# Flags of the unused slots read in a nest: GpSimd's additions of expert results in a two-layer graph and mixture-of-experts kernel

## The reference

```python
xn = _layernorm(x)
x = x + L0_gnn(xn, src, dst, ...) + L0_mix(xn)
x = x + L0_ffn(_layernorm(x))        # 8 experts, each row goes to the best 2
xn = _layernorm(x)
x = x + L1_gnn(xn, edges, edge_weight, ...) + L1_mix(xn)
x = x + L1_ffn(_layernorm(x))        # 1 shared expert for all rows, and 8 of which each row takes 2
```

## Time and profile before

| | us |
|---|---|
| median of 3 runs | 2321.13 (2317.22 to 2322.07) |
| the profiled execution, its own time | 2329.73 |
| its span, first to last instruction | 2328.1 |
| TensorE busy | 2124.0 (91%) |
| VectorE busy | 1713.4 (74%) |
| ScalarE busy | 1231.5 (53%) |
| GpSimd busy | 397.7 (17%) |
| mean granted clock of TensorE | 0.958 of full speed |

### The profile page before, as it was taken

One profiled execution on the slowest core, in us unless ns is written; L12 is line 12 of the kernel. 1 busy time (PEld: TensorE's weight loads), 2 busy tenths in 40 slices (PEclk: granted clock), 3 DMA queues, 4 the chain that ended last, 5 costly groups with the idle time before them and its releaser, 6 DMA issues. The chain is left out here.

```text
span 2328.1 us, 47346 instructions
## 1 busy us (share of the span) xinstructions
PE 2124.0 (91%) x18181; PEld 1978.3 (85%) x18181; DVE 1713.4 (74%) x3516; ACT 1231.5 (53%) x2864; POOL 397.7 (17%) x327
## 2 busy tenths in 40 slices
PE   4768999999868999995999999999998999999996
PEld 2458999999758999994778899989987999999996
DVE  5689778778388888885666566556656887888885
ACT  4376555555425766674541444444435225766674
POOL 4000000000024444443000000000000032444444
PEclk9888999999978999997898999999999999999998
DMA  4143333333444877787100666456642015877786
GB/s 133 60 122 87 87 107 95 87 100 102 145 141 153 229 234 232 222 226 194 29 1 24 187 189 188 129 166 188 188 127 96 24 58 164 233 233 227 224 225 167
DMA packets 236910, 338.91 MB, mean 146 GB/s; under 512 B 29305, under 2 KB 198342, under 8 KB 236550
## 3 DMA queue, kind: packets, MB, share of 16 engines
q1 hardware_dynamic: 208800, 296.14, 40.6%
q0 software_dynamic: 24432, 35.68, 8.6%
q10 hardware_dynamic: 3446, 3.97, 0.5%
HBM read 258.83 MB, written 76.90 MB: 144 GB/s over the span
## 5 line engine op out<-in xcount | busy, mean ns | idle before, releaser
L2306 PE MATMUL bank<-WB_r,XN_r 128*128 128x448 f32 x1400 | 399.7, 367 | 3.7 <-DVE WB_r L2265 3.7
L2265 DVE TENSOR_TENSOR WB_r<-WB,WB_r 128x448 fp32r<-128x448 f32 x350 | 214.0, 624 | 166.2 <-ACT WB_r L2258 166.1
L2258 ACT CAST WB_r<-WB 128x448 fp32r<-128x448 f32 x350 | 197.7, 568 | 222.2 <-PE bank L2306 217.7
L2306 PEld LDWEIGHTS bank<-WB_r,XN_r 128*128 128x128 f32 x1400 | 263.2, 188 | 26.8 <-DVE wb__r L2231 4.4
L1860 PE MATMUL bank<-SC_r,WB_r 128*128 128x256 f32 (+1 forms) x2064 | 254.8, 283 | 12.1 <-issue 9.3
L1860 PEld LDWEIGHTS bank<-SC_r,WB_r 128*128 128x128 f32 x2064 | 248.5, 191 | 16.6 <-issue 16.6
L1044 ACT CAST WB_r<-bank 128x200 fp32r<-128x200 f32 x391 | 137.8, 352 | 196.4 <-PE bank L1028 194.4
L1875 PE MATMUL bank<-R_r,H_r 128*128 128x256 f32 x1752 | 214.0, 280 | 4.6 <-DVE R_r L1771 4.6
L1875 PEld LDWEIGHTS bank<-R_r,H_r 128*128 128x128 f32 x1752 | 207.8, 188 | 4.9 <-issue 4.9
L1724 ACT ACTIVATE wb_<-bank,WB 128x256 f32<-128x256 f32 (+1 forms) x344 | 133.3, 476 | 97.3 <-issue 63.4
L1860 PE MATMUL bank<-SC_r,XN_r 128*128 128x256 f32 x1392 | 169.6, 280 | 4.2 <-issue 3.3
(11 more groups left out here) (436 smaller groups left out, 5305.4 us busy)
## 6 DMA issues: line engine op xcount, KB each, us to landing
WB<-adjw SPq DMA_DIRECT2D x350, 224.0 KB, 2.8
WB<-in_f_pack SPq DMA_DIRECT2D x127, 512.0 KB
WB<-in_f_pack SPq DMA_DIRECT2D x62, 640.0 KB
adjw<-X SPq DMA_DIRECT2D x24, 1600.0 KB, 7.6
WB<-in_f_pack SPq DMA_DIRECT2D x65, 516.0 KB
xd<-XN SPq DMA_DIRECT2D x15, 640.0 KB, 5.5
y<-X SPq DMA_DIRECT2D x10, 640.0 KB, 3.3
X<-y SPq DMA_DIRECT2D x6, 640.0 KB, 6.4
```

The lines of the kernel that those rows point to most:

```text
L2258: e.copy(split_w(m)[0], RAW[m % PR]).then_inc(S("whigh"), 1)
L2265: e.tensor_tensor(al, RAW[m % PR], ah.bitcast(F32), ALU.subtract).then_inc(S("wlow"), 1)
L2306: mm_ = e.matmul(conv_bank(k, band, c)[:, 0:PW], x[st][:, o], y, start=(st == 0 and i == 0), stop=(st == T - 1 and i == 2))
```

## The change

On GpSimd the late slots (25 and up) become a recursive nest of conditionals. In the branch for "used", the slot's two additions are issued, and then, inside that branch, the gather and the flag of the next slot follow, without waiting for the landing and without the write into `mark`. The landing of a late slot is now read from the transfers' own semaphore (`late0`, `late1`, 32 for each slot) by whoever needs it: the next addition, and VectorE before it reuses a buffer. In the branch for "unused", GpSimd waits for all late additions of the layer, counts up a new semaphore `landed` once, and issues the gathers that are left; flags of later slots aren't read. SyncE waits for `landed` at the two places above. The tile `mark` and the semaphore `added` are gone. Nothing of the other engines' handling of the slots changes.

```diff
-        late = (NSLOT - SURE) * L + max(n - SURE, 0)
-        if late:
-            e.wait_ge(S("added"), late)
-
-    def add_pool(e, L, i):
+        if n > SURE:
+            e.wait_ge(S(f"late{L}"), 32 * (n - SURE))
+
+    def wait_all_added(e, L):
+        e.wait_ge(S("add"), 32 * SURE * (L + 1))
+        e.wait_ge(S("landed"), L + 1)
+
+    def add_pool(e, L, i, sem):
         s = L * NSLOT + i
-
-        def rows_of_slot(sem):
-            wait_added(e, L, i)
-            for q in range(2):
-                e.wait_ge(S("obs"), 2 * s + q + 1)
-                e.indirect_dma_start((Y, out)[L], ..., yob[s % 2][:, q, :], None, compute_op=ALU.add).then_inc(S(sem), 16)
-
-        def run():
-            rows_of_slot(f"late{L}")
-            e.wait_ge(S(f"late{L}"), 32 * (i - SURE + 1))
-            e.memset(mark[:, :], 0.0).then_inc(S("added"), 1)
-
-        if i < SURE:
-            rows_of_slot("add")
-        else:
-            if_used(e, L, i, run, lambda: owed(e, "added", (NSLOT - SURE) * L + i - SURE, 1))
+        wait_added(e, L, i)
+        for q in range(2):
+            e.wait_ge(S("obs"), 2 * s + q + 1)
+            e.indirect_dma_start((Y, out)[L], ..., yob[s % 2][:, q, :], None, compute_op=ALU.add).then_inc(S(sem), 16)
+
+    def landed_pool(e, L, n):
+        if n > SURE:
+            e.wait_ge(S(f"late{L}"), 32 * (n - SURE))
+        e.sem_inc(S("landed"), 1)
+
+    def late_pool(e, L, i):
+        if i == NSLOT:
+            landed_pool(e, L, i)
+            return
+        if i + 4 < NSLOT:
+            gather_pool(e, L, i + 4)
+        e.wait_ge(S("used"), 2 * L + 2)
+        o = L * NSLOT + i
+        with e.If(e.value_load(filled[0:1, o:o + 1], min_val=0, max_val=1)):
+            add_pool(e, L, i, f"late{L}")
+            late_pool(e, L, i + 1)
+        with e.Else():
+            landed_pool(e, L, i)
+            for j in range(i + 5, NSLOT):
+                gather_pool(e, L, j)
 
     def slots_pool(e, L, stored):
         gather_pool(e, L, 1)
-        for i in range(NSLOT):
-            if i + 2 < NSLOT:
-                gather_pool(e, L, i + 2)
+        for i in range(SURE + 2):
+            gather_pool(e, L, i + 2)
             if i == 2:
                 stored()
             if i >= 2:
-                add_pool(e, L, i - 2)
-        add_pool(e, L, NSLOT - 2)
-        add_pool(e, L, NSLOT - 1)
+                add_pool(e, L, i - 2, "add")
+        late_pool(e, L, SURE)

     def fetch_sp(e):
-        wait_added(e, 0, NSLOT)
+        wait_all_added(e, 0)
...
         wait_out(e)
-        wait_added(e, 1, NSLOT)
+        wait_all_added(e, 1)
```

More of the change, by code:

```diff
@@ L141, in program @@
     filled = sb("filled", [1, 2 * NSLOT], I32)
-    mark = sb("mark", [1, 1])
     slot_i = sb("slot_i", [128, 2 * NSLOT], I32)
@@ L1940, in wait_added @@
             e.wait_ge(S("add"), 32 * sure)
-        late = (NSLOT - SURE) * L + max(n - SURE, 0)
-        if late:
-            e.wait_ge(S("added"), late)
-    def add_pool(e, L, i):
-        s = L * NSLOT + i
-        def rows_of_slot(sem):
-            wait_added(e, L, i)
-            for q in range(2):
-                e.wait_ge(S("obs"), 2 * s + q + 1)
-                e.indirect_dma_start((Y, out)[L], bass.IndirectOffsetOnAxis(ap=slot_i[:, 2 * i + q:2 * i + q + 1], axis=0),
-                                     yob[s % 2][:, q, :], None, compute_op=ALU.add).then_inc(S(sem), 16)
-        def run():
-            rows_of_slot(f"late{L}")
-            e.wait_ge(S(f"late{L}"), 32 * (i - SURE + 1))
-            e.memset(mark[:, :], 0.0).then_inc(S("added"), 1)
-        if i < SURE:
-            rows_of_slot("add")
-        else:
-            if_used(e, L, i, run, lambda: owed(e, "added", (NSLOT - SURE) * L + i - SURE, 1))
+        if n > SURE:
+            e.wait_ge(S(f"late{L}"), 32 * (n - SURE))
@@ new lines, in wait_all_added @@
+    def wait_all_added(e, L):
+        e.wait_ge(S("add"), 32 * SURE * (L + 1))
+        e.wait_ge(S("landed"), L + 1)
+    def add_pool(e, L, i, sem):
+        s = L * NSLOT + i
+        wait_added(e, L, i)
+        for q in range(2):
+            e.wait_ge(S("obs"), 2 * s + q + 1)
+            e.indirect_dma_start((Y, out)[L], bass.IndirectOffsetOnAxis(ap=slot_i[:, 2 * i + q:2 * i + q + 1], axis=0),
+                                 yob[s % 2][:, q, :], None, compute_op=ALU.add).then_inc(S(sem), 16)
```

## The result

| | before | after |
|---|---|---|
| median of 8 runs, us | 2319.78 (2317.22 to 2322.07) | 2312.78 (2307.2 to 2315.99) |
| ratio, with its 95% interval | | 0.9972 (0.9963 to 0.9981) |
| span of the profiled execution, us | 2328.1 | 2310.0 |
| mean granted clock | 0.958 | 0.961 |

A forecast was written before the change was run, and what follows sets the result against it. TensorE, busy 91% of the span, was taken as the bound, so GpSimd edits count only in two tails: 3.45 us in layer 0 plus 1.55 in layer 1, 5.0 off 2321.13, gives 2316.1 us, range 2311.5 to 2321.0.

The forecast's parts named there:

- Where the time is: GpSimd's late slots: marks delayed only two additions, the last of each layer, so the change acts on two tails.
- Part 1: Late slots before the last one: landing wait, mark and flag leave GpSimd's path, gathers go out sooner; gain 0.
- Part 2: Last addition of each layer: mark, flag and branch leave between landing and issue; 1.0 us in layer 0, 0.75 in layer 1.
- Part 3: End of layer 0: mark and skipped slots' flags leave between last landing and SyncE's fetch; 2.45 us won, bounds 1.6 to 2.65.
- Part 4: End of layer 1, landing to drain: 1.8 us shrinks to about 1.0 with five exit jumps; 0.8 won, bounds 0 to 1.7.
- a stall at the jumps: Layer 1's five exit jumps on GpSimd at 2.23 us each add 10.3 us: 5.3 lost, 2326.4 us; chance 0.10.
- The drain: End of layer 1: drain of 2.61 us may run from the last transfer on, hiding the gain there; 2316.9 us; chance 0.12.
- The clock's rise: Behind layer 0: rise to full clock stays put, half of 3.45 us is lost; 3.3 won, 2317.8 us; chance 0.15.
- more is won: Jumps without cost (0.8 us more) or an earlier clock rise (up to 1.7): about 6.6 won, 2314.5 us; chance 0.08.

The follow-up runs named there:

- land_first: Changed kernel, but in a used slot GpSimd waits for its additions' landing before the next gather and flag; ratio 0.9983 to the kernel before.
- exits: Changed kernel plus a count of a semaphore nobody reads at the end of each used branch; ratio 0.9981 to the kernel before.
- again: The changed kernel once more, no edit; ratio 0.9972 to the kernel before.
- flags_read: Changed kernel, but flags the nest doesn't read are loaded for nothing between last landing and count of landed; ratio 0.9982 to the kernel before.
- out_first: Changed kernel, but from slot 25 VectorE and ScalarE give slot i-1's output before splitting slot i+2's first weights; ratio 0.9956 to the kernel before.
- lean: Changed kernel with outputs ahead of the next weights' splits and no weight transfers for unused slots; 2305.66 us, ratio 0.9939 to the kernel before.
- l0_only: The nest in layer 0 alone, layer 1 keeping flags in a row, mark and landing wait; ratio 0.9977 to the kernel before.
- no_load: Changed kernel, but SyncE loads weights only if their slot's flag is 1, else counts up their semaphores; ratio 0.9964 to the kernel before.

## Why the prediction was right, and by how much it missed

- *Where the time is*: right. Only two additions and two ends were waiting for marks and flags, and only the two tails changed; between late slots the pace is as it was (12.12 us from 1053.36 to 1065.48).
- *Part 1, the gathers that move cost and give nothing*: not contradicted. Layer 0's landing was 0.86 us shorter in the pair of profiles, but the nine profiles that were sorted by the gather overlap, and the instruction packet sorts them better.
- *Part 2, issue behind the landing*: 1.0 + 0.75 forecast, 1.15 + 0.86 measured. My 0.82 for a wait and the transfer's start was 0.1 too long. The flag did go under the transfer, and `land_first` shows the price when it doesn't.
- *Part 3, end of layer 0*: 2.45 forecast, 2.56 measured (2.69 to 0.13).
- *Part 4, end of layer 1*: 0.8 forecast, 1.56 measured (1.83 to 0.27). This is the term that was mis-sized. It charged five jumps, one for each conditional, and there was one. `exits` shows that the price of a jump was nearly right (0.15 us for 0.17) and their number wrong.
- The stable terms sum to 6.1 us in place of 5.0. The rest up to 6.9 in the profiles is the shorter landing of layer 0, less 0.1 of slightly longer ones. The interval of the ratio reaches from 4.4 to 8.6 us, so 6.1 and 7.0 can't be told apart by it, nor 5.0. The landings' part isn't shown to belong to the change, and that the profiles' 6.9 comes so near to 7.0 is luck: with the landings of `again`, the tails won 4.53 and 3.35 us, 7.9 in all.
- The time was forecast as 2316.1 and is 2312.78. Of the 3.3 us between them 1.4 are the kernel before, whose median went from 2321.13 in three runs to 2319.78 in eight. The gain of 7.0 is above the 6.6 that the range was built for; the scatter allowed on both sides holds it.
- *The rivals*: a stall at the jumps didn't come; GpSimd's branches took 34 to 53 ns in the nest, and its 2 jumps out took 38. The rule of the Trainium skill (Runtime: NRT & Kernel Launch, Instruction fetch mechanics), that a taken branch to a page outside the two-page window waits for a fetch of that page, isn't contradicted by that: no branch of the nest showed a wait, and no run here shows whether one left the window. TensorE's 2227 ns look like such a fetch: in each of the twelve profiles exactly one branch takes over 1 us (1.2 to 2.8), it is TensorE's at the end of layer 0's slots, and a 16 KB packet of the queue `instruction` begins within 1.2 us of it. That the one waits for the other wasn't tried. The drain took 2607 ns whether it started 1.83 or 0.27 us behind the last landing, so it moves with its start. The clock's rise moved along with the work, and 2 us further; "more is won" by the clock, up to 1 us of it, isn't excluded.

## What to carry to other kernels

Where a tail waits for a landing, what the issuing engine does between landing and next issue is paid in full: here 0.9 to 1.2 us for a jump and a flag, and 0.8 for each unused slot that is asked. Read flags while a transfer is on its way, and ask no more once one says "unused". And look at what transfers for work that will not take place do in a tail: in the one profile in which they were issued beside the last but one addition, it took 7.8 us to land. Compare the parts of a tail from one event to the next, not spans: two profiles of one kernel differed by 1 us in a landing and by 2.5 us in the stretch between.

## What the runs showed of the hardware

- A chain of conditionals that all end at one point was left by one jump of 38 ns; with one instruction between the ends each exit took 0.23 us, 0.15 of it the jump (exits).
- GpSimd's drain at the end took 2607 ns in eleven of the twelve profiles and 2686 in one (flags_read, where it also began 0.4 us behind the jump in place of 0.15).
- The second of a pair of accumulating transfers took 2.45 us on GpSimd in place of 1.58 when VectorE's and ScalarE's splits ran beside it (out_first, lean). Whether it is their access to memory wasn't tried.
- The landing of one and the same addition, 128 rows of 1 KB each, took between 3.7 and 7.8 us from its start (7.8 is out_first's, beside 1.07 MB of weights). In the quiet behind the last slot it was 3.7 to 3.8 in every profile but lean, whose layer 0 had 4.05.
- In the ten profiles without moved outputs, landings of the last but one slot that had a 16 KB packet of the queue `instruction` beginning 2.1 to 3.3 us after their start took 4.45 to 5.51 us, the others 3.7 to 4.2. Packets that had ended by 2.6 us lengthened none of the last slots' landings (3.7 to 3.8 in l0_only, flags_read and no_load).
